# Ternary feed-forward on one Trainium2 core: half of the Hadamard transform between two steps of TensorE, half copies ahead of a rounding on ScalarE, and a clip moved from VectorE to ScalarE

## The reference

```python
def act_quant(x):                       # per token, qb = 128
    scale = qb / jnp.clip(jnp.max(jnp.abs(x), axis=-1, keepdims=True), EPS)
    xq = jnp.clip(jnp.round(x * scale), -qb, qb - 1) / scale
def fwht(x): ...                        # normalized Walsh-Hadamard transform over the last dim
def bitlinear(x, w):   return einsum('bsh,oh->bso', act_quant(x), weight_quant(w))
def h_bitlinear(x, w): return einsum('bsh,oh->bso', act_quant(fwht(x)), weight_quant(w))
gate, up = bitlinear(x, w_gate), bitlinear(x, w_up)          # 512 -> 2048
return h_bitlinear(silu(gate) * up, w_down)                  # 2048 -> 512
```

## Time and profile before

| | |
|---|---|
| time, median of 3 runs | 3549.21 us (3537.89 to 3550.49) |
| profiled execution | 3549.66 us, of it a span of 3547.6 us |
| the phase of the change | from about 1088 to 1470 us of the span |
| mean granted TensorE clock over the span | 0.957 |

### The profile page before, as it was taken

How to read it: one execution, slowest core, us unless ns; L and a number is a source line. 1 busy time by engine, 2 the same in 40 slices (tenths; PEclk the granted TensorE clock), 3 DMA queues, 4 the chain that set the end, 5 groups by cost and what they waited for, 6 DMA issues and landing times. The chain is left out here.

```text
span 3547.6 us, 42725 instructions
## 1 busy us (share of the span) xinstructions
PE 3130.4 (88%) x14213; PEld 1831.5 (52%) x14244; DVE 2623.1 (74%) x3494; ACT 1801.9 (51%) x3414; POOL 1416.0 (40%) x956
## 2 busy tenths in 40 slices
PE   7869788999996888699999999999999777998985
PEld 3337544333333555455555555555555356786663
DVE  7855698877765888478777877787777764766886
ACT  5644343666653445465666566655555332664220
POOL 1122288000000000076777777767767544223440
PEclk9879999999998999999999999999999888999997
DMA  4137745222218300255555454445444346665321
GB/s 131 47 117 271 266 121 129 66 57 57 57 30 169 41 1 1 83 175 158 173 172 173 157 172 161 160 157 179 165 158 138 119 166 202 241 249 205 142 72 59
DMA packets 229748, 478.65 MB, mean 135 GB/s; under 512 B 36239, under 2 KB 69647, under 8 KB 213664
## 3 DMA queue, kind: packets, MB, share of 16 engines
q1 hardware_dynamic: 223296, 459.19, 40.9%
q0 software_dynamic: 6240, 16.81, 1.4%
HBM read 387.51 MB, written 92.06 MB: 135 GB/s over the span
## 5 line engine op out<-in xcount | busy, mean ns | idle before, releaser
L2378 POOL TENSOR_TENSOR l2x_inflow<-l2x_dtu,l2x_rows_b 128x512 f32<-128x512 f32 x256 | 419.4, 1638 | 271.2 <-DVE l2x_state L2267 263.0
L178 POOL TENSOR_TENSOR ln_work<-ln_work,minus_half 128x4 f32<-128x4 f32 (+1 forms) x34 | 33.2, 976 | 1037.4 <-DVE ln_work L166 1037.3
L2267 DVE TENSOR_TENSOR_SCAN l2x_state<-l2x_decay,l2x_inflow 128x512 f32<-128x512 f32 x256 | 383.1, 1497 | 16.8 <-ACT l2x_decay L2141 16.8
L1324 DVE TENSOR_REDUCE l1x_mx<-psum 128x2 f32<-128x1024 f32 x256 | 308.3, 1219 | 100.0 <-PE psum L1166 98.5
L2394 POOL TENSOR_TENSOR l2x_y_sum<-l2x_y_sum,l2x_state 128x512 f32<-128x512 f32 x224 | 354.4, 1582 | 33.0 <-DVE l2x_state L2276 33.0
L2076 ACT ACTIVATE l2x_probs<-psum,l2x_soft,l2x_norms 128x512 f32<-128x512 f32 x256 | 195.5, 775 | 320.2 <-DVE l2x_soft L2206 320.2
L1281 ACT ACTIVATE l1x_split<-psum 128x1024 f32<-128x1024 f32 x256 | 262.0, 1025 | 158.7 <-PE psum L1166 158.6
L2276 DVE TENSOR_TENSOR l2x_state<-l2x_state,l2x_rows_c 128x512 f32<-128x512 f32 x256 | 266.8, 1042 | 7.6 <-DMA l2x_rows_c<-l3x_xd_dram 1.1
L126 PE MATMUL psum<-l2x_probs_t,l2x_v_tok 128*128 128x512 f32 x512 | 236.3, 605 | 28.9 <-ACT l2x_probs_t L212 25.9
L126 PE MATMUL psum<-l2x_xt,l2x_wq 128*128 128x512 f32 x512 | 230.9, 594 | 7.7 <-issue 6.2
L126 PE MATMUL psum<-l2x_kt,l2x_qt 128*128 128x512 f32 x512 | 230.5, 593 | 4.0 <-ACT l2x_probs L2076 4.0
(11 more groups left out here) (458 smaller groups left out, 7199.6 us busy)
## 6 DMA issues: line engine op xcount, KB each, us to landing
l2x_rows_b<-l3x_xd_dram SPq DMA_DIRECT2D x256, 256.0 KB, 3.7
l2x_rows_c<-l3x_xd_dram SPq DMA_DIRECT2D x256, 256.0 KB, 3.7
l2w_raw<-l_w SPq DMA_DIRECT2D x38, 1024.0 KB, 7.0
l2x_wkv<-l2x_kv_dram SPq DMA_DIRECT2D x32, 1024.0 KB, 6.9
l2w_raw<-l_w SPq DMA_DIRECT2D x38, 512.0 KB, 4.5
l1x_heads_dram<-l1x_stage SPq DMA_DIRECT2D x32, 512.0 KB, 3.3
l2x_wq<-l_wq SPq DMA_DIRECT2D x16, 1024.0 KB, 7.2
l2x_wo<-l_wo SPq DMA_DIRECT2D x16, 1024.0 KB, 5.3
```

What stands on the lines that cost most here:

```text
L1324: main.drain(dve.tensor_reduce(mx[:, gg % 2, :, j, t], g["psum"][:, b:b + 2, :], AX.X, ALU.max), f"m{n}_0", banks=2)
L2267: dve.tensor_tensor_scan(state[:, s % KEPT, :], decay[:, s % 3, :], inflow[:, s % 3, :], 0.0, ALU.mult, ALU.add).then_inc(scan_done, 1)
L2378: pool.tensor_tensor(inflow[:, s % 3, :], dtu[:], rows_b[:, s % 3, :], ALU.mult).then_inc(inflow_ready, 1)
```

## The change

Three things, and what they bring with them. (1) PE does groups 2 and 3 of the transform between the turned yq and the down products, groups 0 and 1 after them; the order of banks follows. (2) ACT copies banks ha2 and ha3 before its rounding. (3) The clip leaves DVE: ACT forms relu(ROUND + 127 - z) from the rounded z, which is 127 minus the clipped number, and the copy of the turned banks makes 127 minus that again. A column `top` holds the constant ROUND + 127 and is set by POOL.

```diff
--- before.py
+++ after.py
@@ -1486,6 +1486,7 @@
         ys = sb("ys", [P, 4, 6])
         yq, yt = sb("yq", [P, 2, I1], BF16), sb("yt", [P, IC, P], BF16)
         empty = sb("empty", [P, ROW])
+        top = sb("top", [P, 1])
 
         order = []
         for t in range(T1 + 3):
@@ -1496,16 +1497,20 @@
             if t < T1:
                 order += [(f"g{t}_{n}", "act") for n in range(4)]
             if 0 <= t - 3 < T1:
-                order += [(f"yt{t - 3}_{k}", "act") for k in range(2)] + [(f"dn{t - 3}", "dve")]
+                order += [(f"yt{t - 3}_{k}", "act") for k in range(2)]
             if 0 <= t - 1 < T1:
-                order += [(f"ha{t - 1}_{n}", "act" if n >= 2 else "dve") for n in (2, 3, 0, 1)]
+                order += [(f"ha{t - 1}_{n}", "act") for n in (2, 3)]
+            if 0 <= t - 3 < T1:
+                order += [(f"dn{t - 3}", "dve")]
+            if 0 <= t - 1 < T1:
+                order += [(f"ha{t - 1}_{n}", "dve") for n in (0, 1)]
         order += [(f"spare{k}", None) for k in range(-len(order) % 4)]
         ring = Ring(sem, "l1f", (4, 5, 6, 7), order)
         ups = Ring(sem, "l1u", (0, 1, 2, 3), [(f"u{t}_{n}", "dve") for t in range(T1) for n in range(4)])
         (had_in, x_steps, z_steps, x_ready, xq_done, mid_ready, y_scale, y_rounded, yq_done, z_in, scaled) = [
             sem(n) for n in ("had_in", "x_steps", "z_steps", "x_ready", "xq_done", "mid_ready", "y_scale", "y_rounded", "yq_done", "z_in", "scaled")]
         weight_in = [sem(f"weight_in{k}") for k in range(3)]
-        empty_made, emptied = sem("empty_made"), sem("emptied")
+        empty_made, emptied, top_made = sem("empty_made"), sem("emptied"), sem("top_made")
         ln = LayerNorm(g, sem)
         blk = ph.block()
         weights = [w_gate, w_up, w_down]
@@ -1560,17 +1565,17 @@
                         r.fill(product(pe, bank(job, r), [
                             (xqt[:, b % 2, c, s * P:(s + 1) * P], w[:, c, n * BLK:(n + 1) * BLK]) for c in range(DC)]))
 
-            def transform(t):
+            def transform(t, quarters):
                 if t == 0:
                     pe.wait_ge(had_in, 16)
-                for n in (2, 3, 0, 1):
+                for n in quarters:
                     ring.wait_for(pe, 0, free=f"ha{t}_{n}", drained=[f"it{t}_{k}" for k in range(4)])
                     for m in range(4):
                         last = pe.matmul(bank(f"ha{t}_{n}")[:, m * P:(m + 1) * P], mid_t[:, 4 * n + m, :], had[:],
                                          start=True, stop=True)
                     ring.fill(last)
 
-            def down(t):
+            def y_turned(t):
                 pe.wait_ge(yq_done, t + 1)
                 for k in range(2):
                     ring.wait_for(pe, 0, free=f"yt{t}_{k}")
@@ -1578,6 +1583,8 @@
                         last = pe.transpose(bank_bf(f"yt{t}_{k}")[:, m * P:(m + 1) * P],
                                             yq[:, t % 2, (8 * k + m) * P:(8 * k + m + 1) * P], g["ident_bf"][:])
                     ring.fill(last)
+
+            def down(t):
                 if t == 0:
                     pe.wait_ge(weight_in[2], 16)
                 ring.wait_for(pe, 0, free=f"dn{t}", drained=[f"yt{t}_1"])
@@ -1591,9 +1598,13 @@
                 if t < T1:
                     gate_up(t)
                 if 0 <= t - 3 < T1:
+                    y_turned(t - 3)
+                if 0 <= t - 1 < T1:
+                    transform(t - 1, (2, 3))
+                if 0 <= t - 3 < T1:
                     down(t - 3)
                 if 0 <= t - 1 < T1:
-                    transform(t - 1)
+                    transform(t - 1, (0, 1))
 
         @blk.scalar
         def _(act):
@@ -1631,12 +1642,16 @@
             def y_turned(t):
                 for k in range(2):
                     ring.wait_filled(act, 0, f"yt{t}_{k}")
-                    copy(act, "act", ring, f"yt{t}_{k}", yt[:, 8 * k:8 * k + 8, :].rearrange("p c n -> p (c n)"),
-                         bank_bf(f"yt{t}_{k}"))
+                    ring.drain(act.activation(yt[:, 8 * k:8 * k + 8, :].rearrange("p c n -> p (c n)"),
+                                              bank_bf(f"yt{t}_{k}"), ACT.Copy, scale=-1.0, bias=QMAX), f"yt{t}_{k}")
 
             def y_round(t):
                 act.wait_ge(y_scale, t + 1)
                 act.activation(z1[t % 2][:], z1[t % 2][:], ACT.Copy, scale=ys[:, t % 4, 3:4], bias=ROUND).then_inc(y_rounded, 1)
+                act.wait_ge(y_rounded, t + 1)
+                if t >= 2:
+                    ring.wait_filled(act, 0, f"yt{t - 2}_1")
+                act.activation(yq[:, t % 2, :], z1[t % 2][:], ACT.Relu, scale=-1.0, bias=top[:, 0:1]).then_inc(yq_done, 1)
 
             def halves(t):
                 if t >= 1:
@@ -1646,6 +1661,7 @@
                     copy(act, "act", ring, f"ha{t}_{n}", half[:, (n - 2) * BLK:(n - 1) * BLK], bank(f"ha{t}_{n}"))
 
             x_round(0)
+            act.wait_ge(top_made, 1)
             for t in range(T1 + 3):
                 if t % ST == 0 and t < T1:
                     x_turned(t // ST)
@@ -1655,10 +1671,10 @@
                     gate(t)
                 if 0 <= t - 3 < T1:
                     y_turned(t - 3)
+                if 0 <= t - 1 < T1:
+                    halves(t - 1)
                 if 0 <= t - 2 < T1:
                     y_round(t - 2)
-                if 0 <= t - 1 < T1:
-                    halves(t - 1)
                 if t % ST == ST - 1 and t // ST + 1 < NB:
                     x_round(t // ST + 1)
 
@@ -1738,12 +1754,6 @@
                 zst.wait(dve)
                 dve.tensor_scalar(y[:, 3:4], y[:, 2:3], float(k), -QMIN, ALU.mult, ALU.mult).then_inc(y_scale, 1)
 
-            def clip(t):
-                dve.wait_ge(y_rounded, t + 1)
-                if t >= 2:
-                    ring.wait_filled(dve, 0, f"yt{t - 2}_1")
-                dve.tensor_scalar(yq[:, t % 2, :], z1[t % 2][:], ROUND, QMAX, ALU.subtract, ALU.min).then_inc(yq_done, 1)
-
             def down(t):
                 ring.wait_filled(dve, 0, f"dn{t}")
                 ring.drain(dve.scalar_tensor_tensor(g["x"][:, t, :], bank(f"dn{t}"), ys[:, t % 4, 4:5], g["x"][:, t, :],
@@ -1756,8 +1766,6 @@
                     rest(t - 2)
                 if t < T1:
                     middle(t)
-                if 0 <= t - 2 < T1:
-                    clip(t - 2)
                 if 0 <= t - 3 < T1:
                     down(t - 3)
                 b = t // ST
@@ -1771,6 +1779,7 @@
 
         @blk.gpsimd
         def _(pool):
+            pool.memset(top[:], ROUND + QMAX).then_inc(top_made, 1)
             pool.memset(empty[:, 0:D], 0.0).then_inc(empty_made, 1)
             pool.memset(empty[:, D:ROW], 1e9).then_inc(empty_made, 1)
             for b in range(NB):
```

## The result

The changed kernel takes 3516.24 us (median of 8 runs, 3513.63 to 3528.41), the kernel before 3538.41 us beside it (8 runs, 3528.15 to 3550.49): a ratio of 0.994, 95% interval 0.9922 to 0.9957. That is 15 to 28 us less. By the prediction's own bound of 0.5% the side is "faster", to which it gave 0.38. The profiled execution took 3514.03 us, its span is 3512.3.

What follows compares the result with a forecast made beforehand. Neither PE nor DVE alone was taken as the bound, but two loops handing over between them. Gains of 18.2 us less 1.0 for clock and 0.4 for matmul changes, net 16.8, gave 3532.5 us; range 3523 to 3545.

Steps and rivals of the forecast that it cites:

- Iterations 3, 7, 11, 14, 15: Iterations where PE's chain sets the next S: 1.74 us less in each, 8.70 us together.
- S: Mark once per iteration: DVE's first step of `widest`; forecast at T + 7.34 instead of T + 9.08.
- T: Mark once per iteration: PE's first transpose of yq; S + 9.94 if PE came in time, S + 11.03 if it stood.
- 4, 8, 12: Iterations where a batch begins: turned inputs start at T + 9.42 instead of T + 10.54, 3.36 us less together.
- 5, 9, 13: LayerNorm iterations: taking the clip off DVE gains 0.58 us each, not 1.14; 1.74 us together.
- 6 and 10: Quantising iterations, where DVE already waited for PE: 0.05 us lost in each, 0.10 together.
- The end: Iteration 16 and after: last `widest` 4.2 us earlier, last rounding and cut give 0.8 back; 3.4 us less.
- The first rival: DVE's list never the bound, so the gain is the same on every tile: 27 us, time 3522; chance 0.10.
- table loads: Rival: Relu and Silu take turns in ACT's tables, two loads of 1.28 us per tile; 3541, chance 0.05.
- ACT's list reaching PE: Rival: Relu and rounding end after it0 is filled, copies of it late, 12 us lost; 3545, chance 0.05.
- The seams: Rival: new four-byte/bf16 changes on PE and longer T - S eat a third to half, 7 us; 3541, chance 0.15.
- The clock rival: Longer standing before it2 leaves PE at 1.2 GHz through the tile, some 10 us on six tiles; 3596, chance 0.05.

Runs made afterwards that it cites:

- the last version: Changed kernel with DVE's sum into x behind LayerNorm and quantisation, ACT's Relu behind the next batch's rounding, and LayerNorm in two parts; 3495.41 us, ratio 0.9871.

## Why the prediction was right and wrong

**Right: the phase.** By the marks of the profile after, against the terms:

- Iterations 3, 7, 11, 14, 15: S at T + 7.38 (forecast 7.34; before 9.08). From S to S they gained 8.03 us net of the clock; the forecast was 8.70 before its 1.0 for the clock.
- 4, 8, 12: turned inputs at T + 9.34 (9.42), 3.61 us (3.36).
- 5, 9, 13: the sum at T + 6.39 (6.36), 1.63 us (1.74).
- 6 and 10: 0.52 us lost (0.10). Quantisation gained nothing from the clip, as said; the clock took the rest.
- 2: 1.14 (1.14). The end: 3.60 (3.4).

These are 17.5 us, against the forecast's 16.8; the rest of the 17.8 lies mostly before the first S, which no term covers and which differs as much between profiles of one kernel.

The first rival, the same gain on every tile, fell: LayerNorm iterations gave a third of it. So did table loads and ACT's list reaching PE, in this kernel. The seams cost almost nothing: S came 0.04 us later than worked out. The clock rival was right in direction and small: T - S rose from 11.33, 11.18, 10.97, 11.03, 10.90, 10.99 to 11.77, 11.46, 11.07, 11.10, 10.89, 11.01, 0.9 us together, where I had taken 1.0. My sign that the prediction is wrong above 11.4 was set too low. The sum of the rival with the seams was wrong in itself: its 7 us leave 11, which is 3538 and not 3541.

**Wrong: the level and the range.** The step that failed is "From the profiled 3549.66 (span 3547.6) that gives 3532.9; the median of before is 0.45 lower, so 3532.5". It treated a median of three as the kernel's level. Eight runs put it at 3538.41, 10.8 us lower: by chance two of the three are among the three slowest of the eight, and the profiled execution is as slow as they. One stretch of unchanged code behind the phase differs by 9.7 us between two executions. With 3538.4 the same sum gives 3521.6, within 5.4 us of the measured 3516.24. The range came from the unknown costs of the edit alone, though the three runs of before already spread over 12.6 us, nearly as much as the effect. The medians lie 22.2 us apart; the 4.4 beyond the phase's 17.8 are within the interval and not explained.

**Partly wrong: why the Relu helps.** I counted it on DVE's list. In the changed kernel that is right in size, but alone it gave less than nothing, and in the last version 22 us: its worth hangs on whether DVE has a wait behind it, on the wait for ACT that leaves DVE with it, and on the clock at which PE goes on behind its own waits, which no term of mine covered.

## What to carry to other kernels

Where two engines hand over to each other, take one mark on each, write the next mark as a distance from the last, and count an edit only in iterations where its mark is the later one; this gave 17 us of 18 here, where the same gain counted on every tile would have given 27. Where a freed engine waits afterwards (DVE for the down products, 35.9 us), put its independent work ahead of that wait: with the LayerNorm taken in two parts that brought another 23 us. And before a time is forecast from one profile, look how far the runs lie apart: an effect of 17 us needs more than a median of three.

## What the runs showed of the hardware

T - S behind a standing PE was the same within 0.1 us in two profiles of the kernel before and of the changed one (iteration 6: 11.18 and 11.23; 11.46 and 11.52), but not always: the last version had 11.48 and 12.38 in iteration 3. Over all kernels, outside the iterations where a batch begins, it lay between 10.85 and 12.44, and it did not follow the length of the idle time: 11.33 behind 7.59 us in one, 11.95 behind 4.13 us in another. The Relu alone left PE's work as it was and still lengthened T - S by 3.1 us together, through how long, and from when on, the granted clock was low. And in the last version with the clip on DVE the clock fell behind 2.25 us of waiting.
